# Raw expert weights land in their own ring place; four places instead of three, six second-layer pieces up front

## What is computed

```python
t = t + _L0_ffn_ref(_ln_t(t), gate_up_proj, down_proj)      # first layer: 4 experts, tokens dealt out in turn
    gu = jnp.einsum('bgeh,ehd->bged', x4, gate_up_proj)     # 512 -> 2 x 512
    inter = jax.nn.silu(gate) * up
    out = jnp.einsum('bgei,eih->bgeh', inter, down_proj)    # 512 -> 512
x = x + _L1_conv_ref(_ln_c(x), ...)                         # second mixer: a scan of 9 steps, 16 states
t = t + _L1_ffn_ref(_ln_t(t), ...)                          # second layer: 8 experts, top 2 by a router
```

## Time and profile before

| | us |
|---|---|
| three runs | 1230.15, 1225.18, 1233.59 (median 1230.15) |
| profiled execution, first to last instruction | 1232.3 |
| of it: until the first expert matmul | 137.67 |
| first expert layer, half 0 (slots 0 to 95) | 238.21 |
| first expert layer, half 1 (slots 96 to 191) | 278.39 |
| routed experts and output | 578.03 |
| busy: PE / DVE / ACT / POOL | 1052.6 / 732.0 / 474.8 / 385.1 |

### The profile page before, as it was taken

The page is one execution under the profiler, slowest core; times in us unless marked ns, Lnnn a source line. Parts: engine busy times, 40 slices in busy tenths (PEclk is TensorE's granted clock), DMA queues, the critical chain, the costliest instruction groups (busy, mean ns, idle before and its releaser), DMA issues. The chain is left out here.

```text
span 1232.3 us, 18131 instructions
## 1 busy us (share of the span) xinstructions
PE 1052.6 (85%) x5916; PEld 885.8 (72%) x5916; DVE 732.0 (59%) x1414; ACT 474.8 (39%) x987; POOL 385.1 (31%) x304
## 2 busy tenths in 40 slices
PE   6876797789879997797898999889878999999975
PEld 3554697779877786686797767667757888888853
DVE  5777667977556458866485434665448334443326
ACT  3361136422223245224512434733552344443333
POOL 1105136424431115112202333631331443334311
PEclk9976899799889998898989999999988999999985
DMA  8317158666785376656464356552671689986557
GB/s 284 131 54 264 62 168 286 212 216 224 258 269 175 131 272 211 242 187 254 171 240 155 137 203 232 196 193 91 227 257 64 214 323 332 360 327 217 182 215 257
DMA packets 93366, 261.60 MB, mean 212 GB/s; under 512 B 10024, under 2 KB 46856, under 8 KB 77408
## 3 DMA queue, kind: packets, MB, share of 16 engines
q1 hardware_dynamic: 58216, 172.60, 39.2%
q0 software_dynamic: 14912, 49.82, 11.4%
q10 hardware_dynamic: 20152, 38.02, 9.8%
HBM read 168.59 MB, written 91.82 MB: 211 GB/s over the span
## 5 line engine op out<-in xcount | busy, mean ns | idle before, releaser
L611 POOL TENSOR_TENSOR sb_ring<-sb_raw,sb_ring 128x1024 fp32r<-128x1024 f32 x48 | 127.3, 2658 | 249.8 <-ACT sb_ring L1179 222.0
L671 PE MATMUL ps<-sb_xnH,sb_ring 128*128 128x288 f32 x512 | 168.6, 329 | 38.7 <-POOL sb_ring L611 14.6
L964 PE MATMUL ps<-sb_w,sb_xtH 128*128 x344 | 152.8, 444 | 16.1 <-DVE sb_hh L1803 14.2
L634 POOL DMA_INDIRECT y_dram<-sb_ysb,sb_target x86 | 87.5, 1017 | 241.9 <-ACT sb_ysb L1260 224.7
L672 PE MATMUL ps<-sb_xnH,sb_ring 128*128 128x288 f32 x512 | 159.6, 312 | 0.0
L673 PE MATMUL ps<-sb_xnL,sb_ring 128*128 128x288 f32 x512 | 159.1, 311 | 0.0
L1796 DVE TENSOR_TENSOR sb_xtL<-ps,sb_xtH 128x512 fp32r<-128x512 f32 x86 | 59.4, 691 | 138.9 <-ACT sb_xtH L1240 128.5
L966 PE MATMUL ps<-sb_w,sb_xtH 128*128 x344 | 138.3, 402 | 0.0
L965 PE MATMUL ps<-sb_w,sb_xtL 128*128 x344 | 137.5, 400 | 0.0
L671 PEld LDWEIGHTS ps<-sb_xnH,sb_ring 128*128 128x128 f32 x512 | 104.2, 203 | 46.1 <-POOL sb_ring L611 15.6
L672 PEld LDWEIGHTS ps<-sb_xnH,sb_ring 128*128 128x128 f32 x512 | 104.7, 205 | 2.7 <-issue 2.6
(11 more groups left out here) (243 smaller groups left out, 2322.1 us busy)
## 6 DMA issues: line engine op xcount, KB each, us to landing
w_dram<-sb_ring SPq DMA_DIRECT2D x48, 1024.0 KB, 6.8
sb_w<-w_dram SPq DMA_DIRECT2D x48, 1024.0 KB
sb_ring<-w_dram SPq DMA_DIRECT2D x24, 1024.0 KB, 7.6
sb_raw<-in_w_ffn SPq DMA_DIRECT2D x24, 512.0 KB, 4.4
sb_raw<-in_w_ffn SPq DMA_DIRECT2D x48, 256.0 KB, 4.7
sb_X<-in_x SPq DMA_DIRECT2D x16, 576.0 KB, 8.7
xn_dram<-sb_XN ACTq DMA_DIRECT2D x18, 512.0 KB
sb_g<-y_dram ACTq DMA_DIRECT2D x18, 512.0 KB
```

The costliest lines, as they stand in the source:

```text
L611: pool.tensor_tensor(to[:, 1, :], raw[:, r % 2, :], to[:, 0, :].bitcast(f32), ALU.subtract)\
L634: pool.indirect_dma_start(y_dram[h], bass.IndirectOffsetOnAxis(ap=target[:, h, m:m + 1], axis=0), ysb[:, r, :], None).then_inc(y_stored[r] ...
L671: pe.matmul(out_ap, w[0], xh, start=start, stop=False)
L964: pe.matmul(PS[:, 1, :], xtH[:, i % 2, k, :], wh, start=k == 0, stop=False)
```

## The change

The ring has four places, and the separate raw buffer is gone: raw data lands in the low half of its own ring place, ACT copies it to the high half, and POOL subtracts in place. SBUF use is the same (2 + 2x3 = 8 rows of 1024 values before, 2x4 = 8 now). A raw load must therefore itself wait for its ring place, and ACT no longer does. All SP traffic of the ring is one generator: loads at the scheduled slot, stores `STORE` = 6 slots behind it; the parting on ACT and POOL stands `PART` = 3 slots behind it (0 for the first four places). The list of slots is new: six pieces before the first block instead of three, ten in the first half instead of eight, eight in the second instead of thirteen. ACT's first copy of the routed stage waits for the last stores of the ring.

```diff
-RING = 3
+RING = 4
+PART = 3
+STORE = 6
@@ ring_schedule
-    blocks = [((-18, -16, -14)[q] if q < AHEAD else 4 * q - 7, q, None) for q in range(2 * HB)]
-    pieces = [(-24 + 2 * i, None, i) for i in range(3)]
-    pieces += [(10 * i + 14, None, 3 + i) for i in range(8)]
-    pieces += [(FFN + 6 * i + 2, None, 11 + i) for i in range(13)]
+    blocks = [(2 * q - 12 if q < RING else 4 * q - 11, q, None) for q in range(2 * HB)]
+    pieces = [(-24 + 2 * i, None, i) for i in range(6)]
+    pieces += [(8 * i + 14, None, 6 + i) for i in range(10)]
+    pieces += [(FFN + 10 * i + 4, None, 16 + i) for i in range(8)]
...
-            free = before[0] + 5 if before[1] is None else block_used(before[1])
+            free = before[0] + 9 if before[1] is None else block_used(before[1])
@@ sync
-                dst = raw[:, r % 2, :]
+                dst = raw[:, i % RING, 1, :]
...
-            def raw_pieces():
-                for r, (slot, q, n, i) in enumerate(splits):
-                    yield slot + 1
-                    sp.wait_ge(lo_done, r + 1)
-                    if r + 2 < len(splits):
-                        load_raw(r + 2)
-                    to = w1_dram[n] if q is None else w0_dram[q]
-                    sp.dma_start(to, ring[:, i % RING, :, :].bitcast(f32)).then_inc(ring_stored[i % RING], 16)
+            def weights():
+                parted = 0
+                for i, (slot, q, n) in enumerate(places):
+                    while parted < len(splits) and splits[parted][0] + STORE <= slot:
+                        yield splits[parted][0] + STORE
+                        store_parted(parted)
+                        parted += 1
+                    yield slot
+                    place_free(sp, i)
+                    if q is None or q < HB:
+                        load_raw(split_at[i])
+                    else:
...
@@ gpsimd
-                    yield slot
+                    yield slot + PART * (i >= RING)
...
-                    pool.tensor_tensor(to[:, 1, :], raw[:, r % 2, :], to[:, 0, :].bitcast(f32), ALU.subtract)\
+                    pool.tensor_tensor(to[:, 1, :], raw[:, i % RING, 1, :], to[:, 0, :].bitcast(f32), ALU.subtract)\
@@ scalar
-                    yield slot
-                    act.wait_ge(raw_loaded[r % 2], raw_count(r))
-                    place_free(act, i)
-                    act.activation(ring[:, i % RING, 0, :], raw[:, r % 2, :], ACT.Copy).then_inc(hi_done, 1)
+                    yield slot + PART * (i >= RING)
+                    act.wait_ge(raw_loaded[i % RING], raw_count(i))
+                    act.activation(ring[:, i % RING, 0, :], raw[:, i % RING, 1, :], ACT.Copy)\
+                        .then_inc(hi_done, 1)
...
@@ x_hi
+                if i == 0:
+                    for place in range(len(places) - RING, len(places)):
+                        act.wait_ge(ring_stored[place % RING], stores(place))
```

More of the change, by code:

```diff
@@ L146, in metaformer @@
     split_of = {q: r for r, (_, q, _, _) in enumerate(splits) if q is not None}
+    split_at = {i: r for r, (_, _, _, i) in enumerate(splits)}
     ctx = ExitStack()
@@ L179, in metaformer @@
         ffn = ExitStack()
-        raw = sb("raw", [P, 2, PIECE], f32, ffn)
         first = ExitStack()
@@ L185, in metaformer @@
         xnL = sb("xnL", [P, FC, KC, FN], f32r, ffn)
+        landing = ExitStack()
+        raw = sb("raw", [P, RING, 2, PIECE], f32, landing)
+        landing.close()
         ring = sb("ring", [P, RING, 2, PIECE], f32r, ffn)
@@ L437, in load_raw @@
                     for u in range(2):
-                        sp.dma_start(to[:, :, u, :], src[b, u]).then_inc(raw_loaded[r % 2], 16)
+                        sp.dma_start(to[:, :, u, :], src[b, u]).then_inc(raw_loaded[i % RING], 16)
                 else:
@@ L454, in blocks_again @@
-            def blocks_again():
-                for q in range(HB, 2 * HB):
-                    i, first = place_of[q], place_of[q - HB]
-                    yield places[i][0] + 0
-                    place_free(sp, i)
-                    sp.wait_ge(ring_stored[first % RING], stores(first))
-                    sp.dma_start(ring[:, i % RING, :, :].bitcast(f32), w0_dram[q - HB])\
-                        .then_inc(w0_loaded[i % RING], 16)
+                        sp.dma_start(to[:, n, :, :], src[b - KC, n]).then_inc(raw_loaded[i % RING], 16)
@@ new lines, in store_parted @@
+            def store_parted(r):
+                _, q, n, i = splits[r]
+                sp.wait_ge(lo_done, r + 1)
+                to = w1_dram[n] if q is None else w0_dram[q]
+                sp.dma_start(to, ring[:, i % RING, :, :].bitcast(f32)).then_inc(ring_stored[i % RING], 16)
+            def weights():
[6 more added lines that the diff above has]
+                    yield slot
+                    place_free(sp, i)
+                    if q is None or q < HB:
+                        load_raw(split_at[i])
+                    else:
+                        first = place_of[q - HB]
+                        sp.wait_ge(ring_stored[first % RING], stores(first))
+                        sp.dma_start(ring[:, i % RING, :, :].bitcast(f32), w0_dram[q - HB])\
+                            .then_inc(w0_loaded[i % RING], 16)
+                while parted < len(splits):
+                    yield splits[parted][0] + STORE
+                    store_parted(parted)
+                    parted += 1
@@ L501, in _ @@
             load_images(1)
-            load_raw(0)
-            load_raw(1)
-            beside = [Beside(part) for part in (raw_pieces(), blocks_again(), second_layer(), first_expert())]
+            beside = [Beside(part) for part in (weights(), second_layer(), first_expert())]
             for s in range(FIRST, 2 * FFN):
@@ L1175, in high_parts, with raw_count @@
                 for r, (slot, q, n, i) in enumerate(splits):
-                    yield slot
-                    act.wait_ge(raw_loaded[r % 2], raw_count(r))
-                    place_free(act, i)
-                    act.activation(ring[:, i % RING, 0, :], raw[:, r % 2, :], ACT.Copy).then_inc(hi_done, 1)
-            def raw_count(r):
-                return sum(16 if splits[i][1] is None else 32 for i in range(r % 2, r + 1, 2))
+                    yield slot + PART * (i >= RING)
+                    act.wait_ge(raw_loaded[i % RING], raw_count(i))
+                    act.activation(ring[:, i % RING, 0, :], raw[:, i % RING, 1, :], ACT.Copy)\
+                        .then_inc(hi_done, 1)
+            def raw_count(i):
+                return sum(16 if q is None else 32 for _, q, _, k in splits if k % RING == i % RING and k <= i)
             def norm_rows(n, c):
```

7 lines of the change are left out of this document (3 added, 4 removed).

## The result

The changed kernel takes 1219.25 us (median of 5 runs, 1218.07 to 1226.05); the kernel before, run beside it, 1233.59 (5 runs, 1225.18 to 1234.86). The ratio is 0.9891, with a 95% interval of 0.9861 to 0.9921: faster by 1.1%, some 14 us. I had forecast 24.4 us, 1206. The sign was right, the size was not: a little over half of it came. 1219.25 lies above the range of the forecast itself (1192 to 1218), just inside that of the rival in which the gains are hidden (1218 to 1242).

What follows compares the result with a forecast made beforehand. PE bounds the first expert layer, standing 32.5 us for late ring places; gains 13.8 (half 0) plus 13.6 (half 1), less 3.0 of costs, net 24.4: 1206 us. Forecast's own range 1192 to 1218; 8 in 10, 1190 to 1226.

Steps and rivals of the forecast that it cites:

- the rival in which the gains are hidden: Gaps go, but time comes back elsewhere, DVE bounding wherever a mixer runs: 1221, range 1218 to 1242; chance 0.18.
- item 3: End of the half 0 mixer: two partings no longer stand ahead of the copy PE's upsampling waits for; gain 1.9.
- items 6 to 8: Half 1 gaps: slot 96, 2.3; slot 120, 4.0 with clock; slots 128 and 132, 2.3 plus 1.0; 3.3.
- The clock's part: Behind a gap PE runs at 1.2 GHz, not 2.4; 1.7 or 3.4 us come back when it goes.
- item 1: Slot 24: gap of 4.27; next late is DVE's low part of expert 1's inputs; gain 2.3, no clock.
- the lock: Four subtractions moved into the last 17 us before slot 0 can hold DVE: 1.0 charged, ends 0 and 9.6.
- item 8: Slots 128 and 132, beside the second layer's scan: 2.3, half the gaps, plus 1.0 for fewer subtractions colliding with scans.
- Item 2: Slots 25 to 47, beside the mixer: two gaps, DVE's busy time allowing 4.0 at most; gain 2.0, ends 0 and 4.0.
- Items 4 and 5: Slot 72, 2.3, and slot 88, 0.5; slot 92, whole gap of 3.06 and 1.7 of clock: 4.8.
- Item 9: Slot 176, routing chain ending half 1: ACT's 4.00 wait for a store goes as piece 23 is parted later; gain 4.0.
- ScalarE's stands: ACT waits for raw data before silu: charged 2.0, ends 0 and 8; sign: waits of 20 us or more without PE's.

Runs made afterwards that it cites:

- a_cut4: Changed kernel with each POOL subtraction cut into 4 instructions of 256 columns (quarters): 1207.3 us, ratio 0.9787.
- a_dve: Changed kernel with the 38 subtractions from slot 8 on done by VectorE instead of GpSimd, one slot later: 1209.3 us, ratio 0.9811.
- a_oldlist: Changed kernel with the earlier kernel's list of pieces (3 ahead, 8 and 13): 1228.0 us, ratio 0.9942.
- a_cut2: Changed kernel with each POOL subtraction cut into 2 instructions of 512 columns (halves): 1217.7 us, ratio 0.9882.

## Why the prediction was right, and where it failed

**Right.** The holes and their owners: 18.7 and 13.8 us of waits, of which 3.3 and none are left. The end of the mixer (item 3): 2.1 for 1.9. The reload gaps, items 6 to 8: 4.2 at the seam (2.8 ahead of slot 96, 1.4 in it), 4.2 at slot 120, 3.5 at 128 and 132, against 2.3, 4.0 and 3.3 in the sum. The clock's part of it came as well: slots 120 and 121 took 5.7 us before, at a granted clock of 0.50 for most of it, and 4.2 now at 1.00. Half 1 as a whole gave 10.9 of 13.6. The prologue came 1.1 us sooner, within 3 us of its old length.

**Right by luck:** item 1. At slot 24, 2.3 us were gained and PE idles 1.97, as forecast, but not for what I named. In the changed kernel PE starts when DVE has added to X; the low part that I named is the one for the second block of tokens, and it ends at 196.02, after PE's start:

```profile
187.38 2.45 DVE L1751 TENSOR_TENSOR sb_xr<-sb_xr,sb_rmb 128x1152 f32<-128x1152 f32 x1
...
193.23 1.19 DVE L1777 TENSOR_TENSOR sb_X<-sb_X,ps 128x576 f32<-128x576 f32 x1
194.33 1.69 DVE L1758 TENSOR_TENSOR sb_xnL<-sb_xr,sb_xnH 128x1152 fp32r<-128x1152 f32 x1
```

```profile
194.57 0.37 PE L683 MATMUL ps<-sb_xnH,sb_ring 128*128 128x288 f32 x1 [1.97 <-DVE sb_X L1777]
```

The same addition ended at 193.44 before. It is 1 us later now, and the row at 187.38 shows where that began: this operation took 1.34 before and meets a subtraction now (186.21 to 188.61).

**Failed, the decisive step:** "The parting's own instructions stay 48 on ACT and 48 on POOL, of the same shapes, so no busy time goes. What moves is their distance to the use." No busy time went, but some came. The change also moved the subtractions against DVE's work, and I priced the lock only for four of them in the prologue (1.0), with 9.6 as the far end, having read its size in the earlier trace rows myself. In the layer, where 38 stand, it stayed at nothing, but for the 1.0 of item 8, which I took as a gain. Measured: 34.1 - 26.9 = 7.2 us more on DVE in half 0, and in half 1 no less for eight subtractions than for thirteen (186.44 and 185.26 us busy). What counts is PE: its idle time in half 0 for parts fell by 15.4 us, and that for DVE's other work rose by 18.8 (table of half 0). `a_cut4` and `a_dve`, which change nothing but these subtractions, show what whole subtractions on POOL cost there: half 0 is 226.8 and 228.9 instead of 238.3. That the first is near the forecast's 238.2 - 13.8 + 2.0 = 226.4 is partly chance, since with quarters the locks are 15.9 us, well under the 26.9 of the kernel before, which I had left standing in every item. Where the locks are about as large as before, 28.4 and 25.0 us by the same reckoning, half 0 is 236.5 (`a_oldlist`) and 231.6 (`a_cut2`). So locks are shown as what holds half 0 up; how much of it the move made, and how much had been there and hidden behind PE's waits for parts, is not shown.

**Item 2** counted 2.0 of at most 4.0; none came: slot 44 starts at 250.06 where it did at 250.32 (`issue` wait of 5.4 us). **Items 4 and 5:** the whole gap of slot 92, for which I said "nothing else is late in the down part", turned into 2.50 us for DVE's addition to X, and at slot 72 two waits for the statistics (1.63 and 3.60) took the place of 3.56. **Item 9:** 4.0 counted for ScalarE's wait. DVE's chain does start 3.7 us sooner relative to slot 175 (2.6 us behind its start instead of 6.3), as forecast; but piece 23's subtraction, moved off ScalarE's path, now stands in that chain and takes 2.2 of it back. What is left is the 1.5 by which slot 191 is further ahead than slot 175 (10.8 and 9.3). PE was as much as 15.8 ahead at slot 180, and lost the difference again, since the chain ends this half. **ScalarE's stands** (2.0): 2.6 us of waits for raw data in half 0, 5.1 in half 1, without a stand of PE that I could lay to them; not the 20 us that I had named as a sign. The sign was wrong, since in most slots the landing was covered. **Item 8's** last term, 1.0 for five fewer subtractions, is not in DVE's busy time.

Of the rivals, "the gaps go, and the time comes back elsewhere" is nearest, at 1221 in its sum; its reason (DVE is the bound wherever a mixer runs) is part of it. DVE was in the way where no mixer runs, too, and there as in the mixer it was held by subtractions.

**Open:** why halves gain so much less than quarters; how the list's 8.7 us divide, as the profiles show only 2 to 6 of them; where most of the 10 us lie that the cut costs in the kernel before; whether a list laid out around DVE's two-input operations would do as well as the cut.

## What to carry to other kernels

When a wait is removed by doing something earlier, ask what each moved instruction runs beside at its new place and whether the two hold each other up, and price that for all of them, not for the few that catch the eye. Time that an engine loses unseen, behind somebody else's wait, comes to light when that wait goes. A long background instruction that can lock out short ones on the critical engine is better cut (here 4 x 256 columns), or done by the locked-out engine itself; but only where its own end is not what is waited for, as the same cut costs 10 us in the kernel before. And a list of prefetches has two ends: what stands behind it in each queue it passes (POOL's statistics, SP's reloads) can move by a whole round.
